# A graph attention kernel on one core: self loops counted once per bank, and the order of two source tiles at each head's turn

## The reference

```python
x1 = relu(x @ W_ah + b_ah)
# gat_conv, for three weight sets W0, W1, W2, all on the same x1:
h = (x1 @ W).reshape(N, H, C)
as_n, ad_n = (h * a_src).sum(-1), (h * a_dst).sum(-1)
e = leaky_relu(as_n[src] + ad_n[dst], 0.2)
m = segment_max(e, dst); p = exp(e - m[dst]); s = segment_sum(p, dst)
out = segment_sum((p / s[dst])[:, :, None] * h[src], dst).reshape(N, H * C) + b
# the whole
y = relu(concat([relu(out0), relu(out1), relu(out2)]) @ W_out + b_out)
result = layernorm(x + y)
```

## Time and profile before

| | |
|---|---|
| median of 3 runs | 964.36 us (963.82 to 965.69) |
| profiled execution, its time | 963.98 us |
| profiled execution, its span | 962.4 us |
| PE busy | 937.6 us of the span |
| DVE busy | 739.8 us of the span |
| ACT busy | 366.8 us of the span |

### The profile page before, as it was taken

The page is one execution under the profiler, slowest core; times in us unless marked ns, Lnnn a source line. Parts: engine busy times, 40 slices in busy tenths (PEclk is TensorE's granted clock), DMA queues, the critical chain, the costliest instruction groups (busy, mean ns, idle before and its releaser), DMA issues. The chain is left out here.

```text
span 962.4 us, 14549 instructions
## 1 busy us (share of the span) xinstructions
PE 937.6 (97%) x5662; PEld 869.3 (90%) x5662; DVE 739.8 (77%) x1064; ACT 366.8 (38%) x534; POOL 45.8 (5%) x94
## 2 busy tenths in 40 slices
PE   6999999999999999999999999999999999999997
PEld 2677649999999999999999999999999879999996
DVE  6999986999999299989989988988877282243233
ACT  1566322122212245465555555555555450011000
POOL 4600000000000000010010010010010100000000
PEclk9999999999999999999999999999999999999999
DMA  6350722534442822153252362239331263223211
GB/s 181 55 183 19 259 85 91 165 115 143 140 153 89 229 82 82 64 126 79 84 120 62 93 130 58 78 87 375 101 103 60 87 169 129 81 85 113 75 33 32
DMA packets 57692, 108.16 MB, mean 112 GB/s; under 512 B 14012, under 2 KB 41245, under 8 KB 56486
## 3 DMA queue, kind: packets, MB, share of 16 engines
q1 hardware_dynamic: 39188, 66.22, 22.7%
q0 software_dynamic: 5360, 18.77, 8.0%
q10 hardware_dynamic: 13090, 22.44, 7.5%
HBM read 80.34 MB, written 27.08 MB: 112 GB/s over the span
## 5 line engine op out<-in xcount | busy, mean ns | idle before, releaser
L1311 PE MATMUL ps<-R_W 125*125 125x193 f32 x2400 | 397.8, 327 | 5.0 <-ACT R_XIN L722 3.9
L1311 PEld LDWEIGHTS ps<-R_W 125*125 125x125 f32 x2400 | 391.3, 188 | 8.7 <-ACT R_XIN L722 7.6
L707 ACT ACTIVATE R_W<-R_EXP,s 125x1250 f32<-125x1250 f32 x120 | 161.2, 1344 | 162.3 <-PE ps L1311 93.9
L998 DVE SCALAR_TENSOR_TENSOR R_W<-R_W,R_CNT 125x1250 f32<-125x1250 f32 x120 | 174.4, 1453 | 3.9 <-DVE R_EXP L987 2.0
L957 DVE CUSTOM_DVE_ANT_0 R_ROWS<-R_MASK,R_ROWS 125x1250 bf16<-125x1250 bf16 x100 | 138.6, 1453 | 3.2 <-ACTq L660 3.2
L1228 PE MATMUL ps<-Wl_hi,x_hi 128*125 128x384 f32 x360 | 122.1, 339 | 0.0
L1228 PE MATMUL ps<-Wl_hi,x_lo 128*125 128x384 f32 x360 | 121.7, 338 | 0.0
L1228 PE MATMUL ps<-Wl_lo,x_hi 128*125 128x384 f32 x360 | 121.6, 338 | 0.0
L1370 PE MATMUL ps<-Wo_hi,xs_hi 128*125 128x384 f32 (+2 forms) x324 | 109.5, 338 | 0.3 <-PE ps L1360 0.3
L1370 PE MATMUL ps<-Wo_lo,xs_hi 128*125 128x384 f32 (+2 forms) x324 | 109.4, 338 | 0.0
L1370 PE MATMUL ps<-Wo_hi,xs_lo 128*125 128x384 f32 (+2 forms) x324 | 109.2, 337 | 0.0
(11 more groups left out here) (146 smaller groups left out, 854.0 us busy)
## 6 DMA issues: line engine op xcount, KB each, us to landing
xs_dram<-R_XIN POOLq DMA_DIRECT2D x18, 625.0 KB, 9.3
h_dram<-R_HOUT ACTq DMA_DIRECT2D x30, 336.0 KB
R_W<-h_dram SPq DMA_DIRECT2D x12, 840.0 KB
R_ROWS<-as_dram SPq DMA_DIRECT2D x12, 625.0 KB, 4.4
R_EXP<-u_dram SPq DMA_DIRECT2D x6, 1250.0 KB, 6.4
R_X<-u_dram SPq DMA_DIRECT2D x6, 1250.0 KB, 5.8
R_ROWS<-in_W_all SPq DMA_DIRECT2D x18, 384.0 KB, 3.5
Wo_sb<-in_W_out POOLq DMA_DIRECT2D x1, 6912.0 KB, 27.3
```

Source lines behind the costliest of these rows:

```text
L707: nc.scalar.activation(prob[r % PSLOTS], expo[:, r % XSLOTS], ACT.Exp, bias=s02[:, r % NT, ds(2 * p + r // NT, 1)]).then_inc(S["exp_done"], 1)
L998: nc.vector.scalar_tensor_tensor(out=prob[r % PSLOTS], in0=prob[r % PSLOTS], scalar=HUGE, in1=cntT[:, r % NT, 0:N], op0=ALU.min, op1=ALU.m ...
L1311: ins = mm(ps[0:PT, o:o + HW], prob[r % PSLOTS][:, t * PT:(t + 1) * PT], hB[:, q, j], start=(j == 0 and t % 2 == 0), stop=(j == NT - 1), s ...
```

## The change

In `unit` the matmul of the self loops leaves the loop over ranges. It is done once for a whole bank, after the second of the bank's two units (and after the last unit), with one more matmul wherever a tile border falls into the bank: 36 matmuls in place of 114, with up to 48 moving columns in place of up to 12.

In attention, `tile` is split. At source tile 0 of a head only the own columns (4 to 9) are done. At source tile 1 PE waits for its `p_ready`, does its own columns, then the shared columns of tile 0 with the two waits for ACT, signals `p_used` for tile 0, does the shared columns of tile 1 and signals `p_used` for it. From tile 2 on nothing changes. The number of products is the same.

```diff
@@ in unit(u)
-                    edge_products(acc_cols(w), ones[:, u % ONES, i * each:(i + 1) * each], CPW, w % 4 == 0, False)
-                    own = acc_cols(w).rearrange("p (x j) -> p x j", j=NT)
-                    d0, d1 = w * WD, min(w * WD + WD, N)
+                    ins = edge_products(acc_cols(w), ones[:, u % ONES, i * each:(i + 1) * each], CPW, w % 4 == 0, False)
+                if u % 2 or u == NU - 1:
+                    b0, b1 = BANKS[u // 2]
+                    own = bank(u // 2 % 2)[0:PT, 0:(b1 - b0) * MC].rearrange("p (x j) -> p x j", j=NT)
+                    d0, d1 = b0 * WD, min(b1 * WD, N)
                     cuts = sorted({d0, d1} | {d for d in range(PT, N, PT) if d0 < d < d1})
                     for a, z in zip(cuts, cuts[1:]):
                         ins = mm(own[:, a - d0:z - d0, a // PT], ident16[0:PT, 0:PT], ident16[0:PT, a % PT:a % PT + z - a],
@@ new, before tile
+            def columns(p, q, j, ts):
+
+                for t in ts:
+                    o = out_at(q, t)
+                    ins = mm(ps[0:PT, o:o + HW], prob[(q * NT + j) % PSLOTS][:, t * PT:(t + 1) * PT], hB[:, q, j],
+                             start=(j == 0 and t % 2 == 0), stop=(j == NT - 1), skip_group_check=True)
+                return ins
@@ in tile(p, r)
-                for t in OWN_FIRST:
-                    if j == 0 and t == 4:
-                        pe.wait_ge(S["out_evac"], NT * (2 * p + q) + 1)
-                        if q == 1:
-                            pe.wait_ge(S["attT_sb"], 9 * p + 1)
-                    if j == 0 and t in (0, 2):
+                if j == 0:
+                    pe.wait_ge(S["out_evac"], NT * (2 * p + q) + 1)
+                    if q == 1:
+                        pe.wait_ge(S["attT_sb"], 9 * p + 1)
+                if j < 2:
+                    columns(p, q, j, range(4, NT))
+                if j == 1:
+                    for t in (0, 2):
                         pe.wait_ge(S["out_evac"], NT * (2 * p + q) + t + 3)
-                    o = out_at(q, t)
-                    ins = mm(ps[0:PT, o:o + HW], prob[r % PSLOTS][:, t * PT:(t + 1) * PT], hB[:, q, j],
-                             start=(j == 0 and t % 2 == 0), stop=(j == NT - 1), skip_group_check=True)
-                ins.then_inc(S["p_used"], 1)
+                        ins = columns(p, q, 0, (t, t + 1))
+                    ins.then_inc(S["p_used"], 1)
+                if j >= 1:
+                    columns(p, q, j, OWN_FIRST if j > 1 else range(4)).then_inc(S["p_used"], 1)
```

## The result

The changed kernel takes 956.16 us (median of 6 runs, 955.51 to 956.70), the kernel before beside it 964.54 us (6 runs, 963.82 to 965.69): a ratio of 0.9908, interval 0.9898 to 0.9918. That is 8.4 us less; 9.4 were forecast (955.0), and the range of 952.8 to 958.6 holds it. The profiled execution is the longest of the six (956.7 us, span 955.1).

What follows compares the result with a forecast made beforehand. PE was taken as busy 937.6 of 962.4 us, with DVE full in the counting and first pair. 962.4 - 2.4 (self loops) - 7.0 (turns) = 953.0 us span, 954.6 profiled, 955.0 median; range 952.8 to 958.6.

Steps and rivals of the forecast that it cites:

- Edit 1's waiting: Self loops in the counting: DVE's six waits for PE, 2.4 us in all, would all go.
- PE's remaining 2.3 of 4.7 us turns into a wait before the scores that grows from 0.85 to about 3 us: End of the counting: PE's saving beyond DVE's 2.4 us would become idle time ahead of the scores.
- After that DVE runs without a gap: Behind DVE's last wait at 73.97: no gap through the last one-hots and 136 reductions to 129.86.
- Turns 1 and 2: First two head changes in attention: PE 1.96 us ahead after turn 2, a DVE-set wait of some 0.9 us left.
- Turns 3 to 11: Later head changes in attention: nine gaps of PE waiting for ACT all covered, worth 5.0 us.
- The margin of 0.6 us: Turns 4, 6 and 8: the new order's cover would outlast the wait for ACT by 0.6 us.
- Covers too short: Rival at the turns: one cover fails; half of the new order's gain lost, 958.5 us; chance 0.12.
- slower: the slot comes back late: Rival in attention: tile 0 held longer delays tile 5 at 12 heads, 978 us; chance 0.04.
- no change: Rival: the time is given back somewhere in h or in the output stage; chance 0.05.
- The counting gives little: Rival: the self loops gain nothing (957.4 us) or half (956.2), bank evacuation replacing the wait; chance 0.08.
- The clock: Rival: the stop of about 3 us before the scores brings 1.2 GHz, 959 to 963 us; chance 0.04.
- More than I count: Rival: the reductions' gate is not binding, 951.9 us, or about 953 with one edit in full; chance 0.07.

Runs made afterwards that it cites:

- e7: The changed kernel with each reduction over half of its columns: 955.17 us, ratio 0.9897 to the kernel before.
- e2: The kernel before with only the new order at the turns of heads, self loops as they were: 958.56 us, ratio 0.9931.
- e5: The kernel before with no cover: at source tile 0 of a head the shared columns come first: 994.85 us, ratio 1.0305.
- e3: The kernel before with the new order only at turns into the second head of each pair (odd turns): 966.26 us, ratio 1.0008.
- e10: The changed kernel with DVE's fifth masked maximum of each of the first four pairs moved behind `invert`: 955.75 us, ratio 0.9906 to the kernel before.
- e1: The kernel before with only the self loops once per bank, attention as it was: 962.54 us, ratio 0.9975.
- e6: The changed kernel with own columns of three source tiles first: 956.20 us, ratio 0.9912 to the kernel before.
- e8: The kernel before with half the one-hots and half-length reductions, so PE alone sets the counting: 964.46 us.
- e9: The changed kernel with half the one-hots and half-length reductions, so PE alone sets the counting: 953.44 us.

## Why the prediction was right, and where its sizes were off

**What bounds what.** Right. Both edits take time from PE or its gaps, and in both what arrived was set by asking where DVE stands. The end of the counting stage is DVE's, so of PE's 4.7 us (measured 4.5) only DVE's waiting came through, 2.3 us of the forecast 2.4. That these two agree so well is luck in part, as the next two points say.

**Edit 1's waiting.** All six waits should go; three small ones stayed, 0.6 us in all. The list fell by 1.8 us, yet the one-hots' stretch is 2.3 shorter. The difference is a term that the prediction had for PE and left out for DVE: a one-hot lasts 1.20 us, but in an unbroken row the next begins 1.11 us behind it (two take 2.31 us, three 3.42). Each wait therefore costs 0.09 us more than the list says, the six of before 2.96 us and the three of after 0.8; waits under 0.1 us, which the list leaves out, make up the rest. So DVE had over 3 us to lose and lost 2.3 of it. PE's lead at unit 36, worked out as 2.8 us, is less than that.

**"PE's remaining 2.3 of 4.7 us turns into a wait before the scores that grows from 0.85 to about 3 us."** This step failed in size. The idle time grew to 1.46. The prediction let PE keep its whole surplus to the end of the counting, while the ring of three slots lets PE be ahead of DVE only until its next one-hots are missing. PE's waits for one-hots, 1.9 us against 0.5 from 35 to 95 us, show where most of the surplus went, and e7 shows what was left of it: freed of the long reductions, the changed kernel gains 1.0 us. The total is untouched, but whoever had gone on to shorten the reductions would have hoped for 2.3.

**"After that DVE runs without a gap."** Wrong: there was a stop of 1.13 us for a weight load (at 118.61, inside the stretch that the earlier trace rows spans), now 1.50. It took 0.37 us from edit 1 in this pair of executions. That is chance, since in e2 to e5, with the old counting, it was longer than 1.13. Of the prediction's signs, the reductions ended at 128.98, which is 127.94 on the clock of before, for the forecast 127.5.

**Turns 1 and 2.** Right to the step. From the first load of head 0 to the resumption at turn 2 it is 70.02 us in both kernels (339.53 to 409.55, 338.65 to 408.67), with 12 more loads behind PE: 1.96 us ahead. The wait left is 0.76 for a forecast of some 0.9. e3 and e10 show that it is DVE's: with DVE's maximum out of the way it is gone.

**Turns 3 to 11.** The nine stops are gone, as said. They are worth 4.5 us and not 5.0: the sum of 7.0 was 6.45 in the trace, and 6.3 in e2's times. The term that was mis-sized is "each gap costs 0.025 us more than shown". A stretch of 200 loads that begins behind a stop takes 32.65 us; one that begins without a stop takes 32.71, as the row at 372.48 of e3 shows. Nine times 0.06 is the missing 0.54. The trace of before shows where the 0.06 lies (timeline of PE's loads, 375.4 to 375.7 us, the first two loads behind turn 1's stop):

```profile
375.50 0.29 PEld L1311 LDWEIGHTS ps<-R_W 125*125 125x125 f32 x2 [1.36 <-ACT R_XIN L722]
```

Two loads fit into 0.29 us, so the second begins 0.11 us behind the first in place of 0.163. All eleven stops of before are like this. A gap is thus worth its length, plus 0.025, less 0.06: 0.03 us less than shown.

**The mechanism at turns 4, 6 and 8.** The prediction treated turns 3 to 11 as nine separate gains of PE's. e3 showed that the odd ones among turns 3 to 7 are paid out only because the even turn behind them is covered as well. The margin of 0.6 us at these turns was the right thing to look at, and it held: in the changed kernel ACT begins turn 4's evacuation at 475.59, the pieces for the second wait are out by about 476.9, and PE's loads run on without a stop.

**Rivals.** "Covers too short", "slower: the slot comes back late" and "no change" show in no row of the trace: L722's waits are one in place of eleven, and attention has no stop for tile 5. "The counting gives little" did not come (e1: 2.3 us), though the wait for a bank's copy that it named exists, with 0.5 us. "The clock" did not come, since the stop before the scores stayed at 1.46; the mechanism exists all the same, as e3 and e5 show. "More than I count" did not come: 956.16 lies above the forecast, and by e7 the reductions' gate does bind.

**The sum.** Forecast 2.4 + 7.0 = 9.4; the edits alone 2.3 + 6.3 = 8.6; together 8.4. In the traces 1.92 + 6.45: of the 1.0 that is missing, 0.55 is the size of a gap at turns 3 to 11 and 0.37 the longer stop for the weights.

What stays open: why the second load behind a stop comes early, and what delays the weight load of 117 us. Neither was tried.

## What to carry to other kernels

Where two engines are both nearly full, ask for each later gate which engine opens it: what the other one gains is handed to that gate and comes out as a longer wait there (some 0.5 us each at turns 4, 6 and 8 of e3, 1.31 at turn 2), so it is cashed only when that gate is covered too, and a trial of half of such an edit can show nothing. A wait for another engine's evacuation is best covered by work that is there anyway, moved ahead of it. The amount is right when no stop is left; one tile more only moves the stop to where the next input is late (e6).

## What the runs showed of the hardware

- Behind a stop of 2.46 to 3.32 us of PE, in the middle of otherwise unbroken work, the granted clock fell to the 1.2 GHz level in seven of twelve cases (e3 turn 2, e5) and cost 1.6 to 1.7 us each time; five stops of 2.46 to 2.49 us were followed by a clock of 1.00. Behind the shorter stops, up to the 1.46 us before the scores and one of 1.78 us in the counting of before (loads at 25.19), it stayed at 1.00. The Trainium skill, page "TensorE: Matmul & The Clock Gate", section "Why this matters for your kernels", warns of idle gaps between bursts; the rows agree that they can cost more than their length.
- A load and matmul of the identity in f16, 12 columns or fewer, cost 0.058 us each in a full stream, by the pair e8 and e9. In the changed kernel those with up to 48 columns step on by the same 0.06, like the edge matmuls with 120.
- Behind a stop the second weight load begins 0.11 us after the first; in the stream of attention the step is 0.163 (375.50 in before).
- One-hots on DVE last 1.20 us and follow each other every 1.11 us, so a wait between two costs 0.09 us more than its idle time.
